# Unread products beside a serial scan, and the output's products cut into pieces between its steps

## The reference

```python
x = residual + mha(...)                          # x6 + attention: the kernel's x7
U = (layernorm(x) @ W_in.T + b_in) @ Bmat        # 16 x 128 x 64: u, the drive
def step(s, u_t):
    s = silu(s @ A.T) + u_t
    return s, s
states = scan(step, zeros, U over the tokens)    # 128 dependent steps
out = x + states @ Cmat + (program_probs.mean(axis=1) @ W_prog.T + b_prog)[:, None, :]
```

## Time and profile before

| | us |
|---|---|
| median of 3 runs | 904.4 (901.54 to 906.85) |
| the profiled execution, its own time | 900.69 |
| span of the profiled execution | 898.5 |
| PE busy in the span | 752.9 (84%) |
| DVE, ACT, POOL busy | 538.7, 428.9, 336.6 |
| mean granted TensorE clock | 0.913 of full speed |

### The profile page before, as it was taken

One profiled execution on the slowest core, in us unless ns is written; L12 is line 12 of the kernel. 1 busy time (PEld: TensorE's weight loads), 2 busy tenths in 40 slices (PEclk: granted clock), 3 DMA queues, 4 the chain that ended last, 5 costly groups with the idle time before them and its releaser, 6 DMA issues.

```text
span 898.5 us, 16236 instructions
## 1 busy us (share of the span) xinstructions
PE 752.9 (84%) x5488; PEld 608.1 (68%) x5488; DVE 538.7 (60%) x2244; ACT 428.9 (48%) x1760; POOL 336.6 (37%) x343
## 2 busy tenths in 40 slices
PE   0799897799799979997999899979899787575556
PEld 0587676688678858886888688867787576344445
DVE  1558578647847884788478948884876572310003
ACT  0735265565553855385538554781464451312221
POOL 3224263434534552454345533652345251100000
PEclk9899899999999999999999999999999899555556
DMA  8500000100000000000000000000000000010002
GB/s 318 202 7 19 24 13 7 26 1 1 19 1 24 1 19 1 24 1 19 1 24 2 13 1 25 1 1 2 1 1 1 1 2 0 1 24 0 1 0 94
DMA packets 15861, 20.83 MB, mean 23 GB/s; under 512 B 3613, under 2 KB 12322, under 8 KB 15138
## 3 DMA queue, kind: packets, MB, share of 16 engines
q1 hardware_dynamic: 15778, 19.79, 6.7%
HBM read 17.69 MB, written 2.10 MB: 22 GB/s over the span
## 4 chain that ended last, share of the span: by engine, by line
PE 66%; DVE 18%; ACT 5%; issue 5%; POOL 3%; DMA 2%; SPq 1%; DVEq 0%; POOLq 0%
PE work_bank L572 21%; PE work_bank L563 20%; PE scores_bank L771 6%; PE work_bank L701 5%; DVE probsT L1012 4%; DVE probs L911 4%; PE work_bank L555 3%; PE work_bank L621 3%; ACT probs L1153 3%; PE scores_bank L599 2%; DVE xn L929 2%; ACT probs L1090 2%; DVE stats L948 2%; POOL probs L794 1%; DMA bias<-in_mask 1%
## 5 line engine op out<-in xcount | busy, mean ns | idle before, releaser
L794 POOL TENSOR_TENSOR probs<-probs,rtotal 128x512 f32<-128x512 f32 x160 | 164.7, 1042 | 217.9 <-DVE rtotal L1002 217.6
L1090 ACT ACTIVATE probs<-probs,nmx 128x128 f32<-128x128 f32 x512 | 197.9, 390 | 78.8 <-DVE nmx L911 78.4
L1012 DVE COPY probsT<-work_bank 128x512 f32<-128x512 f32 x160 | 106.5, 680 | 16.6 <-PE work_bank L701 16.6
L701 PE MATMUL work_bank<-ident,probs 128*128 128x128 f32 x640 | 97.5, 292 | 21.4 <-POOL probs L794 14.7
L572 PE MATMUL work_bank<-L_w,hidden 128*128 128x256 f32 x512 | 113.9, 380 | 0.0
L572 PEld LDWEIGHTS work_bank<-L_w,hidden 128*128 128x128 f32 x512 | 96.0, 190 | 14.1 <-ACT hidden L1145 1.7
L794 POOL TENSOR_TENSOR rstd<-veps,half 128x2 f32<-128x2 f32 x64 | 45.5, 712 | 158.1 <-DVE veps L956 157.7
L701 PEld LDWEIGHTS work_bank<-ident,probs 128*128 128x128 f32 x640 | 76.4, 149 | 41.4 <-POOL probs L794 22.0
L1090 ACT ACTIVATION_READ_ACCUMULATOR probs<-probs,nmx 128x1 f32 x512 | 97.1, 190 | 0.0
L771 PE MATMUL scores_bank<-probs,a_t 64*64 64x16 f32 x252 | 49.5, 275 | 33.4 <-ACT probs L1153 33.4
L555 PE MATMUL work_bank<-ident,xn 128*128 128x128 f32 x256 | 42.2, 288 | 35.1 <-DVE xn L929 35.1
(11 more groups left out here) (159 smaller groups left out, 1411.6 us busy)
## 6 DMA issues: line engine op xcount, KB each, us to landing
L_w<-in_L_w SPq DMA_DIRECT2D x4, 1024.0 KB, 10.9
x_in<-in_x SPq DMA_DIRECT2D x8, 256.0 KB, 2.8
c_in<-in_ctx SPq DMA_DIRECT2D x8, 256.0 KB, 2.8
cT<-in_ctxT SPq DMA_DIRECT2D x8, 256.0 KB, 3.1
out<-x_all SPq DMA_DIRECT2D x8, 256.0 KB, 2.2
rows<-in_rows SPq DMA_DIRECT2D x1, 1280.0 KB, 7.9
bias<-in_mask SPq DMA_DIRECT2D x8, 128.0 KB, 2.2
L_wq<-in_L_wq SPq DMA_DIRECT2D x3, 256.0 KB, 9.5
```

The source lines that it names most:

```text
L701: mm = nc.tensor.transpose(d[:, j * P:j * P + P], src[:, j, :], ident[:])
L794: return nc.gpsimd.tensor_tensor(out, a0, a1, op)
L1012: nc.vector.tensor_copy(turn_slot(s, i, key), d[:].rearrange("p (j k) -> p j k", j=4))\
L1090: ins = nc.scalar.activation(e_at[slot][:, j, :], src, ACT.Exp, bias=nmx[:, slot, j:j + 1], scale=1.0 if s == "C" else -1.0, accum_out=tot ...
```

## The change

1. `occupy` issues products that nobody reads: 32 columns of weights over 128 rows, 128 columns moving (144 in the scan), each record of the pair overwriting the same place. They stand in pair 7's layer C, 14 ahead of flip x6, 3 ahead of q, 3 ahead of the scores, 14 ahead of turn 0, 2 ahead of turns 1 to 3, mix and out, 14 ahead of flip x7, 4 ahead of drive and 4 behind it; and one behind each scan step up to step 66.
2. The products of A with u come apart: the first ahead of step 1, the others at steps 8, 40 and 72, in place of the unread product.
3. The program means are made in the setup, in `drive_weight`, and `prog` is loaded with the weights. DVE's copy into `stT` follows B7's last product; ACT makes the first w from a tile of zeros, after pair 7's `out`, with the silu's table load.
4. The output's products come in pieces. Tokens 0 to 63 of all batches are done in 32 pieces (64 weight columns, 128 moving) behind the steps 67 to 99 (not 72), tokens 64 to 95 in 28 pieces behind steps 100 to 127 and 4 after the scan. The additions and stores of these tokens follow four pieces each. Tokens 96 to 127 come after the last step, before these 4 pieces, as 16 products with 32 weight columns, laid side by side in four column groups; x7's rows for them were moved by four DMAs into the tile `late`, and `late` is stored by four DMAs, two from SP behind its loop over the 16 other stores and two from ACT.

```diff
+            def occupy(d, n, columns=P):
+                for _ in range(n):
+                    nc.tensor.matmul(d[0:32, 0:columns], wq["L0"][:, 0, 0:32], wk["L0"][:, 0, 0:columns], start=True,
+                                     stop=True, skip_group_check=True)
...
+                if (s, i, step) in OCCUPIED:
+                    occupy(open_bank(s, i, step), OCCUPIED[s, i, step])
...
-            pe.wait_ge(*done("C", NT - 1, "drive"))
-            for n in range(4):
+            def from_u(n):
                 lo = 32 * n - 1 if n else 0
...
+            def last_part(k):
+                n, b, lo = k // 4, k // 2 % B, (k % 2) * P
+                of = slice(0, FIRST) if n < NT else slice(FIRST, FIRST + SECOND)
...
+                mm = nc.tensor.matmul(w_bank[n % W_BANKS][of, at:at + P], stT[:, b, of], w_last[:, lo:lo + P],
+                                      start=True, stop=True)
...
+            ready(exped, EXPED["C", NT - 1, ("exp", 3)])
+            occupy(s_bank[3], 4)
+            pe.wait_ge(*done("C", NT - 1, "drive"))
+            mm = from_u(0)
+            part = 0
             for t in range(1, P):
-                if t == 2:
...
-                    for b in range(B):
-                        means_mm = nc.tensor.matmul(w_bank[3][SS:P, b:b + 1], prog[:, b, :], mean_w[:], start=True,
-                                                    stop=True)
                 if t > 1:
                     pe.wait_ge(silued, t - 1)
                     mm = nc.tensor.matmul(s_bank[t // 32][0:SS, (t % 32) * B:(t % 32) * B + B], a_t[:],
                                           w_state[:, t - 1, :], start=False, stop=True, skip_group_check=True)
                 mm.then_inc(stepped, 1)
...
+                if t in (8, 40, 72):
+                    from_u(t // 32 + 1)
+                elif t < FIRST_FROM:
+                    occupy(s_bank[3], 1, P + 16)
+                if t >= (FIRST_FROM if part < 2 * B else SECOND_FROM) and t != 72:
+                    last_part(part)
+                    part += 1
+
+            pe.wait_ge(states_ready, 5)
+            for g in range(4):
+                for j in range(4):
+                    mm = nc.tensor.matmul(s_bank[g // 2][32 * j:32 * j + 32, (g % 2) * D:(g % 2) * D + D],
+                                          stT[:, 4 * g + j, FIRST + SECOND:P], w_last[:], start=True, stop=True)
...
+            states(0, 32)
+            states(32, FIRST)
+            for n in range(NT - 1):
+                add_last(n)
+            states(FIRST, FIRST + SECOND)
+            before_end = (P - SECOND_FROM) // 4
+            for n in range(NT - 1, NT + before_end - 1):
+                add_last(n)
+            states(FIRST + SECOND, P - 1)
+            states(P - 1, P)
+            add_last(NT + before_end - 1)
+            for k in range(2):
+                add_late(k)
+            for n in range(NT + before_end, 2 * NT):
+                add_last(n)
```

## The result

| | before | after |
|---|---|---|
| median, us | 903.1 (4 runs, 901.5 to 906.9) | 873.9 (4 runs, 872.1 to 875.2) |
| ratio | | 0.968 (95%: 0.965 to 0.971) |
| profiled execution, its own time | 900.7 | 875.2 |
| span of the profiled execution | 898.5 | 873.4 |
| mean granted clock | 0.913 | 0.971 |

The median of before has one run more than the one ahead of the prediction (904.4). The change takes 29 us off. The forecast was 872. The slices of the page of after stand against the earlier trace rows: the clock is full from slice 34 to the end, where it was half.

The account below looks back on a forecast made before the run. Bound: pair 7's serial layer C chain, then the scan at the low clock. Savings of 7.3, 8.7, 9.8 and 4.85 less 0.2 take 30.45 off 900.7, giving 870.2; half of 3.7 added makes 872, range 863 to 897.

Parts of the forecast that it names:

- The bound: Serial chain of pair 7's layer C from 755 us, then the scan at 1.2 GHz; the high clock speeds each link.
- the four terms: Savings in pair 7's chain 7.3 us, between drive and first step 8.7, in the scan's steps 9.8, at the end 4.85.
- Unread products in pair 7: Pair 7's layer C: unread products in PE's waits hold the clock through the chain, saving 7.3 us.
- Between u and the first step: Between drive and scan: one product of A stays, the means move to the setup; 10.46 us becomes 1.7, saving 8.7.
- The step: Scan: a step takes 0.57 us instead of 0.66, bounds 0.55 and 0.66; 9.8 us saved over the scan.
- the third rival: Scan: PE bounds the step as changes of shape cost more than 0.08; 883 us, or 891 with 0.72; chance 0.12.
- The end: Last silu to the span's end: 7.75 us instead of 12.6, saving 4.85, bounds 3 to 6.5.
- The setup and the front: Setup before B0's scores: means covered by PE's wait, only DVE's extra copy counts, 0.2 us lost; loading prog costs nothing.
- The half of 3.7 us: Whole kernel: the median stood 3.7 us above the profiled execution; half was added to 870.2, giving 872.
- The clock isn't held: Pair 7 and scan: unread products fail to hold the clock, PE-bound steps at 0.50; 935 us, chance 0.15.
- The fall at step 67: Scan: the clock falls when the output's pieces take over at step 67; 897 us, chance 0.10.

Follow-up runs that it names:

- The version with another order: Kernel after with 2 instead of 4 unread products behind the last drive and SP's two late stores ahead of its 16th other store: 874.8 us (0.967).

## Why the prediction was right, point by point

- **The bound.** A serial chain at the low clock, so each link is worth what the high clock gives it. Right: taken together the four terms were forecast at 30.65 us less and measured at 30.5 in the two traces. The medians of the whole kernels differ by 29.3.
- **Unread products in pair 7.** 7.3 forecast, 7.47 measured. They were all covered; only the four behind the drive stood in the chain, and halving them gave back the 0.35. But the total hides two errors that nearly cancel. The flip gave 0.32 where 0.5 was forecast. And the earlier turns were put at nothing, while one of them was worth 0.33: ACT's exponentials last 5.7 us in both kernels, but before the change DVE was then still copying the result of a turn, and the reciprocal for the last one had to wait for it. Before, that copy starts at 773.68 and lasts 0.69, the exponentials end at 773.94 and the reciprocal starts at 774.29. In after the copy starts at 775.83, the exponentials end at 776.55 and the reciprocal starts at 776.58.
- **Between u and the first step.** 8.7 and 8.77. The means in the setup cost what DVE's copy costs: in after B0's scores start 0.06 behind DVE's last copy, and PE had done the means (143.9) before the copies began (144.2). From the start of the copies to the scores are 0.69 us instead of 0.39, 0.1 more than the 0.2 put down for it; the scores start at 144.91, where they started at 144.97.
- **The step.** 0.57 and 0.577, by the route that was named: stream, change of shape, load, product, change back. The 0.08 for a change of shape, worked out from 1.92 against 1.73, carried it: what 0.577 leaves for each of the two is 0.09; the two full drains (0.72) that I had joined to the third rival did not come.
- **The end.** 4.85 and 4.35. The last issue started 5.1 behind the last silu, as forecast (5.15). The term that was mis-sized is what follows it: I took the 2.6 us of the stores of before, and it was 3.2, with 512 KB in four stores close together landing after up to 2.8. The version with another order shows that an earlier issue does not shorten this part by much. The 2.6 was the value of one execution, too: in the second profile of before it is 4.5. From the last silu to the end took 8.24 us, where under 8 was forecast as a sign.
- **The setup and the front.** 0.2 forecast and 5.4 in the traces, so the first step product came at 791.9 and not near 787, though B0's scores did not move. The step that failed here is silent in the prediction: it took one execution of before as exact over its first 755 us, and another one of the same kernel was 5.2 us longer there. The half of 3.7 us that I added for the median covered a part of it by luck. Whether the change itself costs some of it (2 to 4 us by the estimate above) stays open.
- **The rivals.** The clock isn't held: didn't come, but its price was right (935 forecast, 931.5 with the clock low from the start). What decided it was what I could not know from the trace: whether 128 rows by 144 columns are enough beside the scan's own 64*64 products. I gave it 0.15; the 96 columns show how near it was, since with a third less streaming in the same products the clock fell at step 8. The prediction names no reason for 144, so that it was enough is in part luck. The fall at step 67 didn't come: pieces with 64 or 32 weight columns over 128 rows and 128 moving columns kept 1.00 up to the end. By the rule quoted in the prediction from the Trainium skill, "TensorE: Matmul & The Clock Gate", table of "Why this matters for your kernels" ("keep TensorE busy"), the clock should have stayed in the three kernels with 64 rows, 96 columns or 128 weight columns, where PE was shown as busy all the time. It fell in each, and the measurement decides. The version without unread products does not speak against the rule: PE was busy 3.13 of the 5.00 us ahead of the fall.

## What to carry to other kernels

A serial stage on PE at the low clock can be sped up by products that nobody reads, if they fit into PE's wait at the high clock. Reckon both: what the chain gains, and PE's own round with two changes of shape; the second is the floor, and at the low clock the same products make the stage slower than without them (0.94 against 0.66 a step here). Start them before the clock falls. Use all 128 rows, which held the clock here where 64 did not, and few weight columns, and try one size less only with a measurement beside it. Look at what else stands in the stage: here the clock of every weaker version fell at the one step where another product took the unread one's place. And before a difference of two traces is put down to a change, profile the unchanged kernel twice.

## What the runs showed of the hardware that I had not expected

- What PE is shown busy with does not tell whether the clock stays. With a product always in flight, unread products of 128 rows by 144 moving columns kept 1.00 over the 38 us of steps 1 to 66. With 64 rows by 144, 128 rows by 96, and 128 rows by 96 with 128 weight columns the clock fell to 0.50 at step 8, each time in or just behind the product of A with u that stands there.
- The same products that kept the clock up did not raise it: 120 us at 0.50 with PE busy 120.00 of 120.00 us.
- One program's first 755 us vary by 5.2 us from one execution to another, and the clock's falls lie at other places. Its last stretch varied by 2.7, 1.9 of it in the landing of the last store.
